# Graph attention kernel on one core: an early half product, accumulators cleared by ScalarE, gathers in another order, and small operations moved inside the attention turns

## The reference, cut to what matters

```python
def gatv2(x, src, dst, Ws, bs, Wd, bd, attn):
    H, D = attn.shape
    fs = (x @ Ws + bs).reshape(-1, H, D)
    fd = (x @ Wd + bd).reshape(-1, H, D)
    e = jax.nn.leaky_relu(fs[src] + fd[dst], 0.2)
    logits = jnp.einsum('ehd,hd->eh', e, attn)
    m = jax.ops.segment_max(logits, dst, num_segments=N)
    ex = jnp.exp(logits - m[dst])
    denom = jax.ops.segment_sum(ex, dst, num_segments=N)
    alpha = ex / denom[dst]
    out = jax.ops.segment_sum(alpha[:, :, None] * fs[src], dst, num_segments=N)
    return jax.nn.elu(out)
```

## Time and profile before

| | us |
|---|---|
| three executions: lowest, median, highest | 3357.31, 3361.42, 3370.45 |
| profiled execution, its own time | 3364.68 |
| its span in the profile | 3363.0 |
| TensorE busy in it | 2863.0 (85%) |
| VectorE busy | 2307.4 (69%) |
| ScalarE busy | 1689.3 (50%) |
| GpSimd busy | 1623.9 (48%) |

### The profile page before, as it was taken

The page is one execution under the profiler, slowest core; times in us unless marked ns, Lnnn a source line. Parts: engine busy times, 40 slices in busy tenths (PEclk is TensorE's granted clock), DMA queues, the critical chain, the costliest instruction groups (busy, mean ns, idle before and its releaser), DMA issues. The chain is left out here.

```text
span 3363.0 us, 59697 instructions
## 1 busy us (share of the span) xinstructions
PE 2863.0 (85%) x13556; PEld 2142.5 (64%) x13557; DVE 2307.4 (69%) x4380; ACT 1689.3 (50%) x5352; POOL 1623.9 (48%) x2067
## 2 busy tenths in 40 slices
PE   5885888888699799998777999999999976777699
PEld 3442444445355455554347999999999874555598
DVE  6536889889766788887575555555555447888743
ACT  0004889889622133332334665656566566777400
POOL 4666666566456555553113555454554445555201
PEclk9897999999999899999788999999999998999899
DMA  4235344444511565555218777777777747666412
GB/s 140 83 82 159 118 133 132 118 133 134 166 38 48 162 170 171 171 171 167 76 63 267 246 240 241 244 238 241 242 242 226 226 142 224 199 213 206 122 34 65
DMA packets 175009, 546.00 MB, mean 162 GB/s; under 512 B 55332, under 2 KB 56344, under 8 KB 174724
## 3 DMA queue, kind: packets, MB, share of 16 engines
q0 software_dynamic: 82000, 370.33, 35.2%
q1 hardware_dynamic: 70596, 122.50, 11.6%
q10 hardware_dynamic: 22304, 52.11, 5.0%
HBM read 461.31 MB, written 83.81 MB: 162 GB/s over the span
## 5 line engine op out<-in xcount | busy, mean ns | idle before, releaser
L2195 PE MATMUL pO<-wh,gT 128*128 128x384 f32 x3264 | 866.1, 339 | 13.2 <-ACT gT L2146 12.0
L805 POOL DMA_INDIRECT row<-fs_d,rec x400 | 456.0, 1140 | 385.2 <-PE pA L1330 159.5
L2195 PEld LDWEIGHTS pO<-wh,gT 128*128 128x128 f32 x3264 | 593.4, 188 | 21.4 <-ACT gT L2146 19.4
L2195 PE MATMUL pO<-wl,gT 128*128 128x384 f32 x1632 | 546.8, 335 | 0.0
L2209 DVE TENSOR_SCALAR cntge<-pT 128x768 int32<-128x768 int32 x137 | 131.2, 958 | 423.4 <-ACT gT L2146 217.1
L1038 ACT ACTIVATE sj<-sj 128x96 f32<-128x96 f32 x1176 | 313.0, 268 | 78.4 <-DVE sj L1155 77.6
L2146 ACT ACTIVATE gT<-cntge 128x256 fp32r<-128x256 f32 x822 | 294.2, 410 | 29.4 <-DVE cntge L2212 4.5
L2195 PEld LDWEIGHTS pO<-wl,gT 128*128 128x128 f32 x1632 | 307.8, 189 | 0.0
L805 POOL DMA_INDIRECT row<-y_d,rec x200 | 203.4, 1017 | 173.7 <-PE pR L2341 115.9
L1077 PE MATMUL pS<-row,ident 128*128 128x384 f32 x400 | 175.8, 523 | 129.3 <-DVE sj L1155 80.6
L2341 PE MATMUL pR<-row,share 128*128 128x384 f32 x384 | 164.3, 580 | 118.4 <-issue 72.9
(11 more groups left out here) (386 smaller groups left out, 5998.1 us busy)
## 6 DMA issues: line engine op xcount, KB each, us to landing
fdt<-in_L_gnn_W_rel_dram SPq DMA_DIRECT2D x170, 384.0 KB
startrow<-seen_d ACTq DMA_DIRECT2D x141, 320.0 KB
raw<-in_L_gnn_W_rel_dram SPq DMA_DIRECT2D x34, 384.0 KB
row<-fs_d,rec POOLq DMA_INDIRECT x400
kept_d<-fdt SPq DMA_DIRECT2D x10, 384.0 KB
kept<-kept_d SPq DMA_DIRECT2D x10, 384.0 KB
fs_d<-of SPq DMA_DIRECT2D x9, 388.0 KB
fd_d<-of SPq DMA_DIRECT2D x9, 388.0 KB
```

Of the source, the lines that this page charges most:

```text
L805: pool.indirect_dma_start(b["row"][u][:, j, :].bitcast(words), None, table, bass.IndirectOffsetOnAxis(ap=b["rec"][u][:, 2 * j + field:2 * ...
L2195: last = pe.matmul(pO[:, q, 0:HALF], gT[:, c, half, :].bitcast(F32R), w[:, c, lo:up].bitcast(F32R), start=c == 0 and k == 0, stop=c == KC ...
```

## The change

Five things are altered, and no arithmetic is added or left out.

1. TensorE, projection: `half(0, 0, P, 0)` with its two waits stands ahead of the 160 one-hot matmuls instead of behind them.
2. GpSimd, first attention: `fd_rows(0)` goes behind the three records, and the nine other `fdt` tiles go between the rows of turn 0 and those of turn 1.
3. First attention: `acc` is no longer cleared by a MEMSET of VectorE. VectorE clears `scaled` first and signals `zero_ok`; ScalarE copies `scaled` eleven times over into `acc` in one operation and signals `acc_ok`, for which VectorE waits ahead of its loop.
4. VectorE, first attention, `weigh`: `dsum` and `den` go ahead of the three long multiplications, with which the turn now ends. A branch for one head that nobody took is dropped.
5. VectorE, second attention: `weigh` is called inside `dot`, between `lin` and the four long multiplications, with which the turn now ends.

```diff
--- before.py
+++ after.py
@@ -544,6 +544,9 @@
 
                     pe.wait_ge(const_built, CONSTS)
                     turn(0, 0, P)
+                    hT_ok.wait(pe, 0, 0)
+                    pe.wait_ge(w_in[0], 16)
+                    half(0, 0, P, 0)
                     pe.wait_ge(onehots, 1)
                     for c in range(EC):
                         last = pe.matmul(p_deg[:, 0:DB], oa[:, c, :], ob[:, c, :], start=c == 0, stop=c == EC - 1)
@@ -552,9 +555,6 @@
                     pe.wait_ge(backs, 1)
                     pe.matmul(p_uns[:, 0:1], ones[0:EP, :], back[:], start=True, stop=True).then_inc(unsorted_sum, 1)
 
-                    hT_ok.wait(pe, 0, 0)
-                    pe.wait_ge(w_in[0], 16)
-                    half(0, 0, P, 0)
                     pe.wait_ge(deg_in, 32)
                     pe.matmul(p_pre[:, 0:NT], lower[:], keycol[:], start=True, stop=True)
                     pe.matmul(p_sum[:, 0:NT], ones[:], keycol[:], start=True, stop=True).then_inc(prefixes, 1)
@@ -808,7 +808,7 @@
         def turns_of(eng):
             return eng.value_load(ctl[0:1, C_TURNS:C_TURNS + 1], min_val=1, max_val=MAX_TURNS)
 
-        def gather_edges(pool, b, table, used, between):
+        def gather_edges(pool, b, table, used, first, others):
 
             pre = Steps(pool, b["pool_step"])
             pre.mark(pool.iota(b["slot"][:], [[1, S], [0, 2]], base=0, channel_multiplier=0, allow_small_or_imprecise_dtypes=True))
@@ -837,12 +837,14 @@
             for u in range(U - 1):
                 record(pre, u, ahead[u])
                 pre.wait()
+            first()
             for u in range(ROWS_AHEAD):
                 pool.wait_ge(b["rec_in"][u], 16)
                 edges_only(u)
                 pool.wait_ge(b["edges_only"][u], 16)
                 rows_of(pool, b, u, table, 0, F32)
-            between()
+                if u == 0:
+                    others()
             PER = 4
             turns = turns_of(pool)
             with pool.Fori(0, turns) as i:
@@ -981,6 +983,7 @@
                 pA = pb("pA", [P, 2, 512], F32, st)
                 pS = [pb(f"pS{j}", [P, 2, 512], F32, st) for j in range(S // 2)]
                 att_in, dve_step, init_ok, fd_first, fd_in = sems(st, "att_in", "dve_step", "init_ok", "fd_first", "fd_in")
+                zero_ok, acc_ok = sems(st, "zero_ok", "acc_ok")
                 sum_ok = Signal(st, "sum_ok", S // 2, U, U)
                 sum_pe = Signal(st, "sum_pe", S // 2, U, U)
                 leaky = Signal(st, "leaky", S, U, U)
@@ -1019,8 +1022,10 @@
                             for t in range(1, NT):
                                 fd_rows(t)
 
-                        fd_rows(0)
-                        gather_edges(pool, b, fs_d[0:1 + N], summed, others)
+                        def first():
+                            fd_rows(0)
+
+                        gather_edges(pool, b, fs_d[0:1 + N], summed, first, others)
 
                     @block.scalar
                     def _(act):
@@ -1039,6 +1044,9 @@
                                                           accum_out=dots[off % U][:, j, h:h + 1])
                                 last.then_inc(logits.sem, 1)
 
+                        act.wait_ge(zero_ok, 1)
+                        act.activation(acc[:], over(scaled[:], 1, [P, NT + 1, D]), ACT.Copy).then_inc(acc_ok, 1)
+                        act.wait_ge(acc_ok, 1)
                         sums(0, 0)
                         turns = act.value_load(ctl[0:1, C_TURNS:C_TURNS + 1], min_val=1, max_val=MAX_TURNS)
                         with act.Fori(0, turns) as i:
@@ -1110,11 +1118,10 @@
                         dve.sem_inc(added.sem, U - 1)
                         PER = 7
                         v = Steps(dve, dve_step)
-                        v.mark(dve.memset(acc[:], 0.0))
+                        dve.memset(scaled[:], 0.0).then_inc(zero_ok, 1)
                         v.mark(dve.memset(den[:], 0.0))
                         v.mark(dve.memset(fdt[:, NT, :], 0.0))
                         v.mark(dve.memset(top[:], -BIG))
-                        v.mark(dve.memset(scaled[:], 0.0))
                         dve.wait_ge(att_in, 16)
                         v.mark(dve.tensor_scalar(attr[:], attr[:], 0.8, None, ALU.mult))
                         v.link(dve.memset(pA[:], 0.0))
@@ -1186,15 +1193,6 @@
 
                             sh = [P, S, heads]
                             ex_ok.wait(dve, i, u)
-                            for j in range(1, S):
-                                if heads == 1:
-                                    ins = dve.tensor_scalar(shares[:, j, :], ident[:], pe_[u][:, 1 + j, :], None, ALU.mult)
-                                else:
-                                    of_heads = row[u][:, j, 0:D].rearrange("p (h d) -> p h d", h=heads)
-                                    ins = dve.tensor_tensor(of_heads, of_heads,
-                                                            over(pe_[u][:, 1 + j, :], 2, [P, heads, HD]), ALU.mult)
-                                ins\
-                                   .then_inc(weighted.sem, 1)
                             v.mark(dve.tensor_reduce(dsum[:], pe_[u][:, 1:S + 1, :].rearrange("p s h -> p h s"), X, ALU.add))
                             d = den[:, ds(tile, 1), 0:heads].rearrange("p o h -> p (o h)")
                             v.mark(dve.tensor_tensor(d, d, pe_[u][:, 0, :], ALU.mult))
@@ -1202,7 +1200,13 @@
                             dve.tensor_tensor(d, d, dsum[:], ALU.add).then_inc(den_ok.sem, 1)
                             assert v.n % PER == 0, v.n
 
+                            for j in range(1, S):
+                                of_heads = row[u][:, j, 0:D].rearrange("p (h d) -> p h d", h=heads)
+                                dve.tensor_tensor(of_heads, of_heads, over(pe_[u][:, 1 + j, :], 2, [P, heads, HD]), ALU.mult)\
+                                   .then_inc(weighted.sem, 1)
+
                         add(0, 0, 0)
+                        dve.wait_ge(acc_ok, 1)
                         dve.wait_ge(fd_in, 16 * (NT - 1))
                         turns = dve.value_load(ctl[0:1, C_TURNS:C_TURNS + 1], min_val=1, max_val=MAX_TURNS)
                         with dve.Fori(0, turns) as i:
@@ -1354,7 +1358,7 @@
                         FIRST = v.n
                         dve.sem_inc(init_ok, 1)
 
-                        def dot(i, off, tile):
+                        def dot(i, off, tile, between=None):
                             rows_wait(dve, b, i, off)
                             fd = of(fdt, tile)
                             for j in range(BY_PE):
@@ -1364,6 +1368,8 @@
                             lin_ok.wait(dve, i, off - 1)
                             dve.tensor_tensor(lin[off % 2][:], row[off % U][:, :, D:W][:, :, 0],
                                               fd[:, D:D + 1].to_broadcast([P, S]), ALU.add).then_inc(lin_ok.sem, 1)
+                            if between is not None:
+                                between()
                             for j in range(S):
                                 if j < BY_PE:
                                     sum_ok.wait(dve, i, off, j + 1)
@@ -1419,8 +1425,7 @@
                                 top_ok.wait(dve, i, u - 1)
                                 arguments(v, i, u, t[u])
                                 count(v, i, u, t[u])
-                                dot(i, u + 1, t[u + 1])
-                                weigh(v, i, u, t[u])
+                                dot(i, u + 1, t[u + 1], lambda: weigh(v, i, u, t[u]))
 
         ahead1 = Ahead("settle1", "L0_gnn_Wos", ("L0_gnn_ln1_w", "L0_gnn_ln1_b"))
         attention("first", HEADS, io["L0_gnn_attn1"], fd_d[0:N], ahead1)
```

## The result

| | before | changed |
|---|---|---|
| median of 20 executions, us | 3367.8 | 3355.61 |
| lowest to highest | 3356.93 to 3372.82 | 3345.38 to 3367.97 |
| profiled execution | 3364.68 | 3360.2 |

The ratio is 0.9967, with a 95% interval of 0.9957 to 0.9977: 11.1 us less, between 7.7 and 14.5. The forecast was 19.5 us less. The time lies in the forecast range, the kernel is faster beyond its interval and stays within half a percent, but the size of the forecast was nearly double.

The account below looks back on a forecast made before the run. VectorE's chain was taken to set the projection, a MEMSET hold on GpSimd the attention opening, VectorE the first loop, TensorE nearly the second. 0 − 8.5 − 3 − 8 = −19.5 us: median 3342 against 3361.4, range 3328 to 3359.

Parts of the forecast that it names:

- A: Projection: moving the first half product ahead of the one-hots was taken as 0, from −3.6 to +4.4 us.
- slack of 3.7: Projection: TensorE's second half product ended at 56.37, 3.7 us before VectorE evacuated it at 60.04.
- The possible 3.6 us at the degree sums: Projection: up to 3.6 us gained if the half product queued behind the degree sums was delaying VectorE's taking them.
- B and C: Opening of the first attention: ScalarE's clear and reordered gathers start the loop earlier, −8.5 us, from −6 to −11.
- D: First attention loop: putting long operations last in a turn hides gaps before lg, −3 us, from 0 to −12.
- the gain of 0.1 us a turn: First loop: about 0.1 us saved before lg in each of three turns in 12 passes, 3.6 us.
- the bound of 0: First loop: the end of the range at which ScalarE's lateness shadows the whole gain from reordering VectorE's operations.
- The pass-top part: First loop: up to 17.4 us of VectorE's pass-top stand, expected to move into its wait for ScalarE.
- E: Second attention loop: long operations last hide VectorE's pass-top stand, −0.85 us a pass, −8 us taken, from +1 to −12.
- TensorE has to follow: Second loop: TensorE's waits for late rows should vanish along with VectorE's stands, −9 us of 11 passes, −8 taken.
- the second rival: Both attention loops: queued work doesn't hide VectorE's pass-top stand; profiled 3358, median 3355, chance 0.08.
- Rival 1: Only the opening of the first attention pays, both loops gaining little; profiled 3355, median 3352, chance 0.22.

Follow-up runs that it names:

- c_alone: Kernel before, with only the clearing of acc moved from VectorE to ScalarE; ratio 0.9994 (0.9985 to 1.0003), opening 65.9 us instead of 67.3.
- memset_twice: Kernel before, with VectorE's MEMSET of acc made twice in a row; GpSimd's IOTA came 8.38 us after its gather, opening 67.2 us.
- fd_last: Changed kernel, with the nine fdt gathers behind the rows of turn 1 again; opening 65.9 us against 65.7.
- no_d: Changed kernel, with dsum and den of the first attention back behind the three long multiplications; first loop 576.6 us against 576.8.
- sum_moved: Changed kernel, with VectorE instead of ScalarE reducing the last edge in the turn behind the pass top; ratio 0.9928 to the kernel before, first loop 555.8 us.
- lib_early: Changed kernel, with one more tiny GpSimd IOTA at the end of its projection work; ratio 0.9941 to the kernel before, opening 59.9 us.
- warm2: Changed kernel, with 95 idle TensorE matmuls before its wait for the first fdt tile and 38 after the first addition; ratio 0.9965 to the kernel before.

## Why the prediction was right or wrong

- **A, forecast 0.** Right. The cold second half took 10.38 us, 2.4 more than 7.99, inside the slack of 3.7. The possible 3.6 us at the degree sums didn't come: VectorE took them at 39.73 instead of 40.31, and near 36 on another chip with and without A.
- **B and C, forecast −8.5: this is the step that failed.** The opening gained 1.6 us. I read the 7.94 us before the IOTA as a hold by VectorE's MEMSET, because the two ends lay within 0.1 us. The MEMSET is worth at most 0.6 (c_alone); the rest is GpSimd's own reconfiguration, which is paid whatever VectorE does. So the gathers of the first rows began some 1.5 us earlier, counted from the end of the projection's last `of`, and not 5 to 8. The section "Who interferes with whom" of "SBUF — State Buffer" in the Trainium skill, which I set beside that row, doesn't cover it: it says that a VectorE instruction with at most one input in SBUF, outside the modes that use both port pairs, doesn't contend with GpSimd, and a MEMSET reads nothing. The runs agree: with no long MEMSET the wait was 7.31, and GpSimd worked beside a MEMSET in memset_twice. The second half of the step, the new order of the gathers, brought the second addition forward by 4.5 us (fd_last), of 5.6 in all, where I had 9 to 12. Against that I had set 3 us for TensorE's late and cold additions, and it was 4.0. The order gave back all but 0.2 us. There was also a slip in the sum: 9 to 12 less 3 is 6 to 9, not 6 to 11.
- **D, forecast −3.** The mechanism was right, but the gain of 0.1 us a turn that I counted as paid was not: the bound of 0 was the truth. The changed kernel's loop is 0.2 us longer than that of no_d, and in the means of the six loops without D and the nine with it D is worth 1 us, less than they scatter. The pass-top part went into the wait for ScalarE, and the 0.1 us a turn went there too, since that wait sets the pass as a whole.
- **E, forecast −8.** Right in mechanism and sign. The mean of five second loops without E is 451.0 us, of fourteen with it 445.6: −5.4. The profiled pair shows −6.4. The term was too large by 2.6 us, and the part that was off is "TensorE has to follow": VectorE's passes became 0.71 us shorter, near the 0.85 of the forecast, but between the starts of TensorE's passes in the same pair it was 37.39 us and is 36.91, only 0.48 less. TensorE's waits for rows, without the one at the loop's end, fell from 7.8 to 3.7 us, so they did hang together with VectorE's stand, and half of them stayed. The stall did hide under queued long operations, so the second rival, drawn from "Instruction fetch mechanics" of "Runtime: NRT & Kernel Launch" in the Trainium skill, fails for VectorE: 0.21 us is left of 1.25. That the stand is such a fetch no run shows.
- **The sum.** 0 − 1.6 − 1 − 5.4 = −8.0 is what the parts account for, inside the measured −7.7 to −14.5. What lies between −8.0 and −11.1 isn't attributed. Of the forecast's surplus over the parts, 11.5 us, B and C make 6.9. That the profiled pair shows only −4.5 is due to the stages behind the second loop, 1777.9 before and 1784.6 after; the profiled execution of before had the shortest relational product of all, 969.3 us against 972 to 983.
- Rival 1 (only the opening pays) was near in its time, 9.5 us less, and by luck: it was E that paid, and the opening hardly did.

## What to carry to other kernels

An idle stretch that ends together with another engine's operation isn't yet caused by it: take the operation away alone before building on it. A gain on one engine in a loop is worth nothing while another engine's late start ends the same turn; look at who is second, by how much, and shift a little work off it in the one turn where it is late, as sum_moved did for 21 us of the loop. And before moving transfers, write down what each of the two consumers then waits for: the new order moved a start by 4.5 us and the result by 0.2. A stand that the profile puts down to nothing may stand elsewhere in the same trace, with other neighbours: look there first.

## What the runs showed of the hardware that I had not expected

- GpSimd stands 6.7 to 8.4 us before its first IOTA or TENSOR_TENSOR behind an operation of another kind (here a reduction over partitions some 150 us earlier), and 6.3 to 7.0 us before that reduction, while MEMSET, COPY, CAST and gathers run without it. A tiny operation of the needed kind, issued ahead of the stage, hides most of it (lib_early: 5.8 us of the opening).
- GpSimd's gather and small operations ran at their usual length beside a VectorE MEMSET of 7.10 us (memset_twice). Beside a VectorE TENSOR_SCALAR of 0.50 us a COPY of GpSimd took 0.90 us instead of 0.18 (before, 260.62).
- One ScalarE copy of 128 x 8448 elements took 7.24 us, 0.86 ns an element, against 0.81 us for 768 (1.05 each).
- While the transfers moved 283 GB/s (283 to 291 us), four records of TensorE's unlooped short matmuls came singly, up to 1.4 us apart, after the first 45 had run at once (warm2); why isn't settled.
